# Row maxima of a causal attention: the corner blocks in banks of their own, their mask added on VectorE

## What is computed

```
q5 = q.reshape(b, reps, KV_HEADS, n, D_HEAD)
scores = jnp.einsum('brknd,bkmd->brknm', q5, k) / scale
causal = jnp.tril(jnp.ones((n, n), dtype=bool))
scores = jnp.where(causal, scores, jnp.float32(-jnp.inf))
p = jax.nn.softmax(scores, axis=-1)
s = jnp.einsum('brknm,bkmd->brknd', p, v)
```

## Time and profile before

| | us |
|---|---|
| median of 3 runs (697.35 to 701.87) | 698.85 |
| the profiled execution, its own time | 692.14 |
| its span, first to last instruction | 690.5 |
| TensorE busy in it | 646.3 (94%) |
| ScalarE | 482.3 (70%) |
| VectorE | 436.3 (63%) |
| GpSimd | 395.1 (57%) |
| mean granted TensorE clock | 0.989 of 2.4 GHz |

### The profile page before, as it was taken

One profiled execution on the slowest core, in us unless ns is written; L12 is line 12 of the kernel. 1 busy time (PEld: TensorE's weight loads), 2 busy tenths in 40 slices (PEclk: granted clock), 3 DMA queues, 4 the chain that ended last, 5 costly groups with the idle time before them and its releaser, 6 DMA issues.

```text
span 690.5 us, 11711 instructions
## 1 busy us (share of the span) xinstructions
PE 646.3 (94%) x3717; PEld 427.4 (62%) x3717; DVE 436.3 (63%) x967; ACT 482.3 (70%) x764; POOL 395.1 (57%) x556
## 2 busy tenths in 40 slices
PE   7999999999999998799999999898999999999994
PEld 5555445655545554468889899775565655555642
DVE  3576759477879789742626544203668888787662
ACT  3777796787987977585444555543989887978563
POOL 5446555657788879803452454155577677725353
PEclk9999999799999999999999999999999999999998
DMA  9059650000000000058878788611111100000003
GB/s 248 1 212 364 225 185 3 15 13 19 19 22 22 19 29 26 26 144 248 264 226 246 211 241 241 194 41 29 31 31 28 31 27 27 17 0 16 16 1 92
DMA packets 66776, 66.46 MB, mean 96 GB/s; under 512 B 7377, under 2 KB 49706, under 8 KB 66714
## 3 DMA queue, kind: packets, MB, share of 16 engines
q1 hardware_dynamic: 60448, 52.62, 25.2%
q0 software_dynamic: 6208, 13.07, 5.9%
q10 hardware_dynamic: 58, 0.02, 0.0%
HBM read 37.31 MB, written 27.85 MB: 94 GB/s over the span
## 4 chain that ended last, share of the span: by engine, by line
PE 54%; POOL 13%; DVE 9%; issue 8%; DMA 7%; ACT 6%; SPq 1%; POOLq 0%; DVEq 0%; ACTq 0%
PE PS L1180 7%; POOL got L2089 5%; PE PS L1042 5%; PE PS L1160 3%; PE PS L1080 3%; DMA got<-expert_rows,IU 3%; PE PS L971 3%; PE PS L977 3%; PE PS L1256 2%; PE PS L991 2%; POOL expert_rows L2061 2%; POOL H L2020 2%; DVE MX L1403 2%; PE PS L983 2%; PE PS L1064 1%
## 5 line engine op out<-in xcount | busy, mean ns | idle before, releaser
L1917 ACT ACTIVATE GF<-PS,XN 128x256 f32<-128x256 f32 (+1 forms) x156 | 68.3, 455 | 63.7 <-PE PS L1160 36.5
L2089 POOL DMA_INDIRECT got<-expert_rows,IU x64 | 65.6, 1025 | 39.5 <-DMA got<-expert_rows,IU 22.2
L2061 POOL DMA_INDIRECT expert_rows<-five,IU x64 | 64.3, 1004 | 40.4 <-DMA expert_rows<-five,IU 17.9
L1180 PE MATMUL PS<-WD,GF 128*128 128x128 f32 x568 | 83.1, 275 | 0.0
L1180 PEld LDWEIGHTS PS<-WD,GF 128*128 128x128 f32 x568 | 75.0, 192 | 1.3 <-ACT GF L1917 0.2
L1042 PE MATMUL PS<-KZ,QS 128*128 128x384 f32 (+5 forms) x192 | 70.8, 444 | 2.6 <-POOL KZ L2041 1.3
L1403 DVE TENSOR_REDUCE MX<-PS 128x4 f32<-128x1024 f32 (+3 forms) x64 | 63.8, 1021 | 13.2 <-PE PS L1043 12.7
L1878 ACT ACTIVATE PA<-PS 128x1024 f32<-128x1024 f32 x64 | 64.9, 1028 | 5.1 <-PE PS L1064 4.9
L2050 POOL TENSOR_SCALAR_AFFINE_SELECT PA<-PA 128x256 f32<-128x256 f32 x128 | 49.1, 415 | 28.2 <-ACT PA L1878 27.9
L2074 POOL DMA_DIRECT2D expert_rows<-YT x39 | 21.7, 557 | 65.3 <-issue 44.6
L2020 POOL TENSOR_SCALAR H<-xc,MOD 128x256 f32<-128x256 f32 x56 | 32.1, 583 | 38.6 <-DVE xc L1363 31.6
(11 more groups left out here) (330 smaller groups left out, 1711.4 us busy)
## 6 DMA issues: line engine op xcount, KB each, us to landing
expert_rows<-five SPq DMA_DIRECT2D x16, 1024.0 KB, 8.7
WU<-in_L_ffn_up_w SPq DMA_DIRECT2D x39, 256.0 KB
WD<-in_L_ffn_down_w SPq DMA_DIRECT2D x39, 256.0 KB
XT<-expert_rows SPq DMA_DIRECT2D x32, 128.0 KB
expert_rows<-YT POOLq DMA_DIRECT2D x32, 128.0 KB, 3.3
BD<-in_L_ffn_down_b SPq DMA_DIRECT2D x39, 64.0 KB
PA<-in_L_attn_x SPq DMA_DIRECT2D x8, 256.0 KB, 5.7
out<-yo SPq DMA_DIRECT2D x8, 256.0 KB, 2.3
```

Source lines behind the costliest of these rows:

```text
L1180: m = pe.matmul(bk[:, b], g[:, b], wd[:, k, :], start=(k == 0 and t == 0), stop=(k == 3 and t == blocks - 1))
L1917: act.activation(GF[slot["gf", kind, u, k]][:, 0:n], bank("up", kind, u, k)[:, 0:n], ACT.Gelu, bias=bias).then_inc(sems["gelu"], 1)
L2061: pool.indirect_dma_start(out=XD[:, :], out_offset=bass.IndirectOffsetOnAxis(ap=IU[:, c, n, k:k + 1], axis=0), in_=HT[c % 2][:, k, :], in_ ...
L2089: pool.indirect_dma_start(out=got[b][n][:, k, :], out_offset=None, in_=XD[:, :], in_offset=bass.IndirectOffsetOnAxis(ap=IU[:, c, n, k:k + ...
```

## The change

1. `UNITS` becomes four pairs of query blocks: (7, 1), (5, 3), (6, 2), (4, 0).
2. `mxm`: the keys of a block ahead of its corner (32i per head) go, for the first three units, both blocks side by side, to one pair of banks (two matmuls a block, two heads each); for the last unit block 4 goes to one bank and block 0 has none. The 32-key corners, one matmul of 128 columns a block, go to a bank `md`, one for two units, four corners in it. All in fp32r; the bf16 mask matmuls and `scores` are gone.
3. `mxr`: one reduce a block over the keys ahead of the corner; after each odd unit an addition of the mask to the four corners of the bank (PSUM and `CM` to a new buffer `JD`), a wait for it, and a reduce of `JD` into a new `MD`. The wait for the masks' load moves from TensorE to VectorE.
4. `mh`: the minimum of the negated `MX` and `MD` twice (rounded, and unrounded into `MN`), then their difference: three instructions for two. GpSimd sets `MX` to 3e38 at the start, for block 0.
5. `place` never gives the two banks of one step twice; the planned times `MXM`, `MXR`, `mh`, `pjm` and `cmb` change; modg(1) is planned behind modg(0); `ORDER1` is a new string. In it modg(1) stands behind the last woh, and plan_tiles(0), plan_bias(0) stay ahead of woh(12). The steps behind the last woh are 370 (371 before). `ORDER2` is the same.

```diff
-UNITS = ((0, 1), (2,), (3,), (4,), (5,), (6,), (7,))
+UNITS = ((7, 1), (5, 3), (6, 2), (4, 0))
...
-MXM = (0.46, 0.3, 0.38, 0.55, 0.6, 0.66, 0.72)
-MXR = (0.54, 0.47, 0.6, 0.74, 0.87, 1.0, 1.14)
+MXM = (0.68, 0.68, 0.68, 0.42)
+MXR = (1.21, 2.35, 1.2, 1.75)
...
-        yield stage("modg", l)
+        yield stage("modg", l, after=[("modg", 0)] if l else [])
...
-        yield stage("mxm", b, u, takes=[(RR, "mx" if u < 3 else "mxw", (b, u), ("mx_red", b, u))],
-                    after=[("kzp", b), ("kza", b)] + [("spe", b // 2, g) for g in range(4)] + ([("mh", b - 2)] if b > 1 else []))
-        yield stage("mxr", b, u)
+        corner = [(RR, "md", (b, u // 2), ("mx_red", b, u + 1))] if u % 2 == 0 else []
+        yield stage("mxm", b, u, takes=[(RR, "mxw" if u < 3 else "mx", (b, u), ("mx_red", b, u))] + corner,
+                    after=[("kzp", b), ("kza", b)] + [("spe", b // 2, g) for g in range(4)] + ([("mh", b - 2)] if b > 1 else [])
+                    + ([("mxm", b, u - 1)] if u % 2 else []))
+        yield stage("mxr", b, u, after=[("mxr", b, u - 1)] if u % 2 else [])
...
+            o = 0
+            for i in UNITS[u]:
+                q, n = QS[c % NQ][:, n0 + i].rearrange("p g n -> p (g n)"), 32 * i
+                if u < 3:
+                    for a in range(2):
+                        pe.matmul(pair("mxw", b, u)[:, a, o:o + 2 * n].rearrange("p (j n) -> p j n", j=2), q, kz[:, 2 * a:2 * a + 2, 0:n],
+                                  start=True, stop=True)
+                elif i:
+                    pe.matmul(bank("mx", b, u).rearrange("p (j n) -> p j n", j=4), q, kz[:, :, 0:n], start=True, stop=True)
+                o += 2 * n
+                m = pe.matmul(d4[:, :, i // 2], q, kz[:, :, n:n + 32], start=True, stop=True)
             m.then_inc(sems["mx_mm"], 1)
-
-        def scores(o, i, q, k, first, last):
-            o = o.rearrange("p (j n) -> p j n", n=32 * (i + 1))
-            js = k.shape[1]
-            pe.matmul(o, q, k, start=first, stop=False)
-            return pe.matmul(o[:, :, 32 * i:32 * i + 32], CM[:, 0:128], CM[:, 128:160].unsqueeze(1).to_broadcast([128, js, 32]),
-                             start=False, stop=last)
...
+            if u % 2:
+                t = own(dve.tensor_tensor(JD[u // 2][:, :].rearrange("p (a n) -> p a n", n=32), bank("md", b, u // 2).rearrange("p (a n) -> p a n", n=32),
+                                          CM[:, 0:32].unsqueeze(1).to_broadcast([128, 16, 32]), ALU.add))
+                w.wait_ge(*t)
+                m = dve.tensor_reduce(MD[b % 2][:, :, 1 - u // 2:8:2], JD[u // 2][:, :].rearrange("p (j a n) -> p j a n", j=4, a=4),
+                                      AX.X, ALU.max, negate=True)
             m.then_inc(sems["mx_red"], 1)
...
-            t = own(dve.tensor_copy(ht[:, 0], mt[:, :, :]))
-            w.wait_ge(*t)
-            dve.tensor_tensor(ht[:, 1], mt[:, :, :], ht[:, 0].bitcast(F), ALU.subtract).then_inc(sems["mh"], 1)
+            md = MD[b % 2]
+            dve.tensor_tensor(ht[:, 0], mt[:, :, :], md[:, :, :], ALU.min)
+            t = own(dve.tensor_tensor(MN[:, :, :], mt[:, :, :], md[:, :, :], ALU.min))
+            w.wait_ge(*t)
+            dve.tensor_tensor(ht[:, 1], MN[:, :, :], ht[:, 0].bitcast(F), ALU.subtract).then_inc(sems["mh"], 1)
```

More of the change, by code:

```diff
@@ L185 @@
+    "H8H8GtH6G7G2H6HzH7H7H6H7H6H7H9H9H7H9H9H+H3G3G4G5H+H+H-H7H+H-GxH-H-H-H-GyGyGyGyGyGyG6"
 )
@@ L227, in free, with place @@
         return (at[0][2], at[0][0]) if at else (None, None)
-    def place(self, done, wide, m=0):
-        at = self.frees(done)
+    def place(self, done, wide, chosen=()):
+        at = [f for f in self.frees(done) if f[2] not in chosen]
         if not wide:
-            return [at[m][2]]
+            return [at[0][2]]
         when = {k: t for t, _, k in at}
@@ L295, in arrange @@
         start = max([x[0], begun] + [done[(s, *k)] + hop for s, *k in after if cost(s, k)[0] != engine])
-        for m, (ring, what, *_) in enumerate(takes):
-            for k in ring.place(done, what in WIDE, sum(r is ring for r, *_ in takes[:m])):
+        chosen = []
+        for ring, what, *_ in takes:
+            for k in ring.place(done, what in WIDE, [k for r, k in chosen if r is ring]):
+                chosen.append((ring, k))
                 ends = [(SIGNALS.get(s, s), wkey) for s, *wkey in ring.ends.get(k, ())]
@@ L787, in program @@
     xin = PT0[1][:, :, :, :].rearrange("p a b n -> p (a b n)").rearrange("p (a k d) -> p a k d", a=NCH, k=4)
-    CM = sb("CM", [128, 160], B16, part)
+    CM = sb("CM", [128, 32], B16, part)
     cin = sb("cin", [16, 2, 128], where=part)
@@ L807, in program @@
     MX = [sb(f"MX{k}", [128, 4, 8], where=part) for k in range(2)]
+    MD = [sb(f"MD{k}", [128, 4, 8], where=part) for k in range(2)]
+    MN = sb("MN", [128, 4, 8], where=part)
+    JD = [sb(f"JD{k}", [128, CH], where=part) for k in range(2)]
     MH = [sb(f"MH{k}", [128, 4, 4, 8], R, where=part) for k in range(2)]
@@ L1390, in mxr @@
             w.wait_ge(*at("mx_mm", b, u))
+            w.wait_ge(zeroed, 5)
+            w.wait_ge(ld_masks, 16)
             if b > 1:
                 w.wait_ge(*at("mh", b - 2))
-            if u < 3:
-                at_ = 0
-                for i in UNITS[u]:
-                    wd = 32 * (i + 1)
-                    m = dve.tensor_reduce(mt[:, :, i], bank("mx", b, u)[:, at_:at_ + 4 * wd].rearrange("p (j n) -> p j n", j=4),
-                                          AX.X, ALU.max, negate=True)
-                    at_ += 4 * wd
-            else:
-                i = UNITS[u][0]
-                wd = 32 * (i + 1)
-                m = dve.tensor_reduce(mt[:, :, i].rearrange("p (a j) -> p a j", a=2),
-                                      pair("mxw", b, u)[:, :, 0:2 * wd].rearrange("p a (j n) -> p a j n", j=2), AX.X, ALU.max, negate=True)
+            o = 0
+            for i in UNITS[u]:
+                wd = 32 * i
+                if u < 3:
+                    m = dve.tensor_reduce(mt[:, :, i].rearrange("p (a j) -> p a j", a=2),
+                                          pair("mxw", b, u)[:, :, o:o + 2 * wd].rearrange("p a (j n) -> p a j n", j=2), AX.X, ALU.max, negate=True)
+                elif i:
+                    m = dve.tensor_reduce(mt[:, :, i], bank("mx", b, u).rearrange("p (j n) -> p j n", j=4), AX.X, ALU.max, negate=True)
+                o += 2 * wd
+            if u % 2:
[4 more added lines that the diff above has]
+                                      AX.X, ALU.max, negate=True)
             m.then_inc(sems["mx_red"], 1)
@@ L2003, in gpsimd @@
             m = pool.memset(MH[k][:, :, :, :].bitcast(F), 0.0)
+        for k in range(2):
+            m = pool.memset(MX[k][:, :, :], 3.0e38)
         m.then_inc(zeroed, 1)
```

82 lines of the change are left out of this document (35 added, 47 removed).

## The result

The changed kernel is slower. Median of 5 runs 707.31 us (705.69 to 714.04), beside 698.62 us of the kernel before (5 runs): a ratio of 1.0147, interval 1.0104 to 1.0191, or 10 us (7 to 13); the medians are 8.7 us apart. The forecast was 696.5 us and "within 1%"; the time came out where the rival "VectorE becomes the bound" had put it (707 us).

What follows compares the result with a forecast made beforehand. The attention stage was taken as bound by no one engine: TensorE leads, VectorE and ScalarE close behind in its second half. Terms -7.5 + 8.8 - 3.7 = -2.4 us, put on 698.85, gave 696.5 us, range 685 to 709.

Steps and rivals of the forecast that it cites:

- VectorE becomes the bound: Rival, attention stage, 140 to 285 us: all 13.6 us of VectorE's added work there appear; +8.1, 707 us; chance 0.22.
- -7.5 (TensorE): Score matmuls of the maxima: 10.9 us saved, times 69%, takes 7.5 us off the path, between 1.3 and 16.8.
- 8.8 (VectorE): Reduces, additions and mh of the maxima: 25.6 us more work puts 8.8 us on the path; bounds 4.4 and 15.6.
- 3.7 (modg): modg(1) leaves its place before plan_tiles(0), where VectorE is the chain: minus 3.7 us, or nothing if other work is late.
- The factor 69%: Of 58.9 us of score and mask matmuls, 40.5 lie on the chain; that share was applied to TensorE's saving.
- half in the dense stretch and 17% outside it: Share of VectorE's added work on the path: 6.8 of 13.6 us in 140 to 285 us, 2.0 of 12 elsewhere.
- Three of the second kind, 1.06: mh's three instructions, priced at 0.353 us each, take 1.06 us a batch, plus 0.2 us over its two before.
- Banks at nothing: Corner banks stay taken over two units, but one pair now serves two query blocks: no cost, some 3 us either way.
- The second part: The work from the last woh to the end (experts, second layer): claimed to take the same time as before.
- The clock rival: A second stretch at 1.2 GHz, 5.2 us of clock lost, on top of the forecast: 702 us; chance 0.10.
- The slower rival: VectorE as the bound, 707 us, chance 0.22; sign: MX reduces and additions pass 12% of the attention stage's chain.

Runs made afterwards that it cites:

- e4: The kernel before without its 192 mask matmuls, maxima counting the masked keys too: 694.97 us, ratio 0.9976 to before.
- e9: The kernel before with 32 mask additions put on VectorE, their result used by nothing: 706.89 us, ratio 1.0148 to before.
- e13: The kernel before with mh in the changed kernel's three-instruction form, same values: 705.32 us, ratio 1.0076 to before.
- e7: The changed kernel with modg(1) moved back in front of plan_tiles(0): 708.01 us, ratio 1.0123 to before.
- e3: The changed kernel without the 32 mask additions, corners reduced straight from their PSUM bank: 700.52 us, ratio 1.0036 to before.
- e11: The changed kernel with each of its 32 mask additions issued twice: 727.51 us, ratio 1.0417 to before.
- e14: The kernel before with two unused small one-input reduces ahead of mh in each batch: 701.65 us, ratio 1.0033 to before.
- e10: The kernel before with modg(1) moved behind the last woh, its scratch tile given its own place: 695.33 us, ratio 0.9967 to before.
- e12: The kernel before without its 192 mask matmuls and with modg(1) behind the last woh: 690.29 us, ratio 0.9873 to before.
- e6: The changed kernel with five fill matmuls ahead of each of the transpose's 16 waits for mh: 716.56 us, ratio 1.0247 to before.
- e8: The kernel before without mask matmuls, planned with fitting times and more fill matmuls, four steps one place later: 703.68 us, ratio 1.0077 to before.

## Why the prediction was wrong

**Which way.** The sum was -7.5 (TensorE) + 8.8 (VectorE) - 3.7 (modg) = -2.4 us. The parts measured, each by itself: -1.7 (e4, for about the same relief), +10.3 and +5.3 (e9, e13), 0 (e7). That is +13.9, where the whole change shows +10 (1.0147 of 698.6). VectorE's two parts are clear of zero; TensorE's and modg's are not. The sum is 4 us too high. The parts don't simply add, and what the new order and the shared banks give back is open within the bound that e3 gives.

**TensorE, the step that failed first.** Two sizes are in it. The relief was priced somewhat low, 10.9 us for some 14, since before's matmuls cost more than the rows that it took. The factor 69% was wrong. It took the score matmuls' share of the chain for the share of a saving that comes back. In e4 13.5 us went and 1.7 came back: 13%, and a third at the far end of its interval. A line that holds 14% of a chain can hold it against others that are nearly as late: VectorE is 74% busy and ScalarE 78%. That this is the reason is argued and not shown, and the clock can have taken up to 4.9 us. The lower bound of the term, 1.3 us, was about right by luck: it stood for a small relief, and the relief was large.

**VectorE.** The work was sized well: additions 0.679 us for 0.685, MD reduces 0.686. What was wrong is the share, half in the dense stretch and 17% outside it. e9 gives nearly half over all batches, where the prediction's 8.8 of 25.6 us is a third, and e11 86% for the next 22 us. A chain's share fails in both directions: too much for a cut, too little for an addition. Added work also pulls the work beside it onto the chain (old reduces from 3.9% to 7.3% in e9). The term's upper bound, 15.6 us, is what e9 and e13 add up to, and that the two agree is chance. It had put most of the cost into 140 to 285 us; in the trace the transpose of batch 7 is already 6.2 us late (155.9 us for 149.7), that of batch 15 15.6 us.

**mh.** "Three of the second kind, 1.06" left out that the time of such an instruction hangs on GpSimd: 1.37 in after and 1.12 in e3 for the same three, 1.06 in e13 only. The Trainium skill ("SBUF — State Buffer", section "Who interferes with whom") says that a VectorE instruction with two SBUF inputs contends with a GpSimd instruction that reads SBUF, that one with at most one such input outside the two-port modes does not, and that reduces never do. The trace agrees: L1419 0.18 to 3.17 us, L1405 and e14's reduces within 14 ns of one length. e14's rounding copy, one SBUF input and up to 1.92 us, must then have been in such a mode; no row tells. And mh isn't work like other work: its end starts a transpose, a copy, a DMA and the scores, so it was wrong to spread it over the stretch at 17% or half.

**modg.** Minus 3.7 us was read from one place in the order where VectorE was the chain. VectorE is the chain there in after too, from 292.1 to 307.4 us. But 1.94 of modg's 3.66 us were one instruction (L1334) that waited for GpSimd, and such a wait doesn't go with modg: in e10 and in after what is behind moved under other work of GpSimd and stretched. 0.7 us are left at the last woh in e10, nothing in after's time (e7).

**What held.** Banks at nothing: TensorE idles 1.8 us ahead of the score matmuls, 2.6 before. The second part is 4.1 us longer in a profiled execution in which it has two stretches at 1.2 GHz; over all the traces it takes 393 to 401 us. The clock rival has a share in it: its sign, a second stretch at 1.2 GHz in this stage, came: there are six for one. In this execution 27.3 us at 1.2 GHz for 10.2 cost at most half of the difference, 8.5 us. The slower rival's time was met by luck, with the TensorE term beside it wrong (-7.5 for -1.7); its mechanism and its sign (16.1% for 12%) were right.

**Where the weights were off.** The trace had the warning: VectorE 84% busy in the dense stretch, and an exchange of 11 us of TensorE for 25 us of VectorE by its own prices (14 for 27 by the traces). That the second engine at 84% hides half of such a load was the hopeful reading; 0.22 for the other was too little.

## What to carry to other kernels

A line's share of the chain tells neither what a cut brings nor what an addition costs: in a stage with several engines at 74 to 95%, taking 14 us from the leader brought 2 us, and adding 22 us to VectorE cost 10, then 19. So don't move work from one full engine to the next at a rate of one to two; look for work that can go altogether, as in e12. A small instruction on a critical hand-over is best a reduce, or one with an input in PSUM, when GpSimd is busy: those didn't wait here, while a minimum of two SBUF tiles, a copy and a `tensor_scalar` did. And a wait seen on TensorE has to be mended where it starts, not filled.

## What the runs showed of the hardware

- An fp32r matmul does not cost by its columns alone. From its start to the next, a corner of 128 columns inside a unit takes 0.06 us (the last of a unit mostly 0.11 to 0.20, to the work behind it), but each of the two of 128 columns ahead of a corner 0.11, those of 64 columns 0.08 and 0.11, the first of 448 columns in a unit 0.28 and the second 0.20. All of them come with a weight load; why the corner is cheapest was not tried.
- A bf16 mask matmul behind its fp32r score matmul takes 0.04 us to the next start in 139 of 192 cases, yet without all 192 of them the same score matmuls take 13.5 us less (e4), 0.07 us a mask.
- The size of the waits between VectorE and GpSimd: up to 3.0 us for an instruction of 0.18 us, and in e10 up to 1.8 us for one of 0.29. Instructions with one SBUF input are among them: a copy 1.92 us for 0.17 (e14), a `tensor_scalar` 2.31 us for 0.32 (L1543, in after and in e7).
- Short fill matmuls are not free even where TensorE waits: 80 of them cost 7 us (e6), 64 of them, with four steps moved, 7 us though the clock rose from 0.93 to 0.99 (e8 against e4).
